# Experts' second products in 256, 304 or 384 columns, picked inside each product, instead of four whole-block forms

## The reference, cut to what matters

```python
scores = softmax(xf @ gate_w.T)            # 8 experts
weights, idx = top_k(scores, 2)            # two experts for each token
h  = einsum('td,eid->eti', xf, w1)         # 2048 -> 1024, each expert
g  = silu(h) * einsum('td,eid->eti', xf, w3)
eo = einsum('eti,edi->etd', g, w2)         # 1024 -> 2048
y  = sum over the two chosen experts of eo * weight
z  = silu(xf @ ws1.T) * (xf @ ws3.T) @ ws2.T   # the shared expert, all tokens
out = x + y + z
```

```
core 0  541 461 502 499 552 505 514 522
core 1  476 500 553 504 504 475 547 537
core 2  512 469 574 478 548 452 505 558
core 3  551 482 509 501 535 467 545 506
core 4  560 450 517 517 592 491 486 483
core 5  529 482 505 525 495 536 516 508
core 6  510 479 542 499 534 528 465 539
core 7  514 507 492 523 562 491 460 547
```

## The kernel before, in words

| rows | form | hidden columns | down tiles |
| --- | --- | --- | --- |
| up to 480 | 0 | one product of 480 | 4 |
| 481 to 512 | 1 | one product of 512 | 4 |
| 513 to 544 | 2 | two of 272 | 5 |
| over 544 | 3 | two of 320 | 5 |

## Time and profile before

### The profile page before, as it was taken

One profiled execution on the slowest core, in us unless ns is written; L12 is line 12 of the kernel. 1 busy time (PEld: TensorE's weight loads), 2 busy tenths in 40 slices (PEclk: granted clock), 3 DMA queues, 4 the chain that ended last, 5 costly groups with the idle time before them and its releaser, 6 DMA issues.

```text
span 2527.0 us, 41508 instructions; the slowest of 8 cores (2481.8 to 2527.0 us)
## 1 busy us (share of the span) xinstructions
PE 2262.4 (90%) x14499; PEld 1310.4 (52%) x14656; DVE 1055.5 (42%) x2142; ACT 710.4 (28%) x1332; POOL 323.8 (13%) x539
## 2 busy tenths in 40 slices
PE   5898999888997999989899999799599879989997
PEld 4555555455544655455444466356256534455443
DVE  5656665666556655555551222021011202111367
ACT  3444442345415553334312102021021202111000
POOL 1111110021101110011111010111011111110331
PEclk8999999999998999999899999899799989989999
DMA  6979887687747876686689698989988696995998
GB/s 101 186 165 214 173 167 176 173 158 128 129 137 172 146 128 119 206 167 121 116 243 225 155 234 159 182 180 178 232 154 176 141 189 144 202 214 119 221 302 320
DMA packets 110734, 445.42 MB, mean 176 GB/s; under 512 B 12416, under 2 KB 12432, under 8 KB 100368
## 3 DMA queue, kind: packets, MB, share of 16 engines
q0 software_dynamic: 76640, 278.47, 62.7%
q1 hardware_dynamic: 33840, 163.59, 18.3%
HBM read 577.84 MB, written 109.05 MB: 272 GB/s over the span
## 4 chain that ended last, share of the span: by engine, by line
PE 67%; DVE 9%; DMA 9%; issue 9%; ACT 5%; DVEq 1%; POOL 0%; ACTq 0%; SPq 0%; POOLq 0%
PE ps L717 24%; PE ps L752 13%; PE ps L446 10%; PE ps L454 7%; PE ps L420 6%; PE ps L431 5%; DVE FW L1101 3%; DMA out<-acc 2%; PE ps L644 1%; DMA gg<-eo,idx 1%; DMA xb<-x_own 1%; DVE Tt L1154 1%; DMA xp<-x_own 1%; DMA out<-y 1%; DMA acc<-y1d 1%
## 5 line engine op out<-in xcount | busy, mean ns | idle before, releaser
L717 PE MATMUL ps<-xg,wr 128*128 128x320 bf16 (+3 forms) x3066 | 488.7, 323 | 80.0 <-issue 76.7
L717 PEld LDWEIGHTS ps<-xg,wr 128*128 128x128 bf16 x3072 | 302.6, 99 | 265.1 <-issue 90.2
L431 PE MATMUL ps<-xT,wq 128*128 128x512 bf16 x978 | 254.7, 402 | 16.3 <-DVE lg L1185 9.8
L1414 DVE TENSOR_TENSOR gb<-sil,ps 128x320 bf16<-128x320 bf16 (+3 forms) x96 | 51.6, 538 | 507.7 <-PE ps L717 507.7
L1580 POOL DMA_DIRECT2D wr<-w_t x240 | 128.0, 546 | 958.2 <-PE ps L717 582.8
L752 PE MATMUL ps<-wr,gb 128*128 128x512 bf16 (+2 forms) x1128 | 247.5, 379 | 3.4 <-issue 1.3
L446 PE MATMUL ps<-wv,xT 128*128 128x256 bf16 x2048 | 232.0, 275 | 3.5 <-ACT xT L808 2.0
L420 PE MATMUL ps<-xT,wk 128*128 128x512 bf16 x983 | 224.4, 380 | 8.7 <-DVE qt L1166 5.0
L454 PE MATMUL ps<-wo,ob 128*128 128x512 bf16 x996 | 225.1, 381 | 2.8 <-issue 0.4
L1025 ACT ACTIVATE sil<-ps 128x320 bf16<-128x320 f32 (+3 forms) x128 | 64.8, 507 | 545.2 <-PE ps L717 535.2
L446 PEld LDWEIGHTS ps<-wv,xT 128*128 128x128 bf16 x2048 | 199.6, 99 | 29.0 <-issue 4.2
(11 more groups left out here) (159 smaller groups left out, 2427.7 us busy)
## 6 DMA issues: line engine op xcount, KB each, us to landing
wr<-w_t POOLq DMA_DIRECT2D x240, 512.0 KB, 19.5
wv<-wv_t POOLq DMA_DIRECT2D x64, 512.0 KB, 8.7
wk<-wk_t POOLq DMA_DIRECT2D x64, 512.0 KB, 10.1
wq<-wq_t POOLq DMA_DIRECT2D x64, 512.0 KB, 7.4
xs<-x2T SPq DMA_DIRECT2D x40, 512.0 KB, 15.0
y1d<-y SPq DMA_DIRECT2D x20, 1024.0 KB, 5.5
xst<-xs SPq DMA_DIRECT2D x40, 512.0 KB, 18.9
eo<-eos SPq DMA_DIRECT2D x40, 512.0 KB, 4.2
```

Of the source, the lines that this page charges most:

```text
L431: ins = t.matmul(self.ps[:, b, :], self.wq[i % 2][:, k * 128:(k + 1) * 128], self.xT[q % 2][:, k, :], start=(k == 0), stop=(k == 15))
L717: ins = t.matmul(self.ps[:, bk, 0:w], self.wr[c % NRING][:, k * 128:(k + 1) * 128], rhs, start=(k == 0), stop=(k == 15))
L1414: v.tensor_tensor(dst, self.sil[n // step % 2][:, 0:w], self.ps[:, self.bank[1, b, ic, s, f], 0:w], OP.mult).then_inc(self.v_g, step)
```

## The change

An expert's hidden columns are now split 256 + 384 in every engine's program, and there is one body for each block. TensorE's first product always has 256 columns. Each second product sits in a small branch (`pe_tail`): 256 columns for up to 512 rows, 304 for up to 560, 384 above. There are 16 such branches in a block, each with three alternatives of 16 matmuls. The gather and the first four down tiles are outside any branch; a fifth tile (`pe_fifth`) is either 32 matmuls or the four small ones. ScalarE and VectorE have no branch left; they always process 256 and 384 columns. The waits for the eight w2 chunks now stand together ahead of the first down product. The fifth tile always has 128 rows; before it had 32 or 128.

```diff
-BLOCKS += [(e, CAP // 128, [(0, CAP // 2), (CAP // 2, CAP // 2)]) for e in range(NX)]
+BLOCKS += [(e, CAP // 128, [(0, 256), (256, CAP - 256)]) for e in range(NX)]
-FORMS = [((0, 480),), ((0, 512),), ((0, 272), (272, 272)), ((0, 320), (320, 320))]
-FTILES = (4, 4, 5, 5)
+WIDTHS = (256, 304, CAP - 256)
...
         for b in range(NB):
+            if 0 < b < NB - 1:
+                self.count = count[b - 1]
+            self.pe_hidden(t, b, BLOCKS[b][2])
             if b == 0:
-                self.pe_hidden(t, b, 0, BLOCKS[b][2])
-                count = self.counts(t)
-                self.pe_xg(t, 0)
-                self.pe_down(t, b, BLOCKS[b][1])
-            elif b < NB - 1:
+                t.wait_ge(self.v_flag, 1)
+                count = [t.value_load(self.rows[0:1, e:e + 1]) for e in range(NX)]
+            if b < NX:
+                self.pe_xg(t, b)
+            self.pe_down(t, b)
+            if 0 < b < NB - 1:
+                mark = len(self.free8)
                 with t.If(count[b - 1] > 512):
-                    with t.If(count[b - 1] > 544):
-                        self.pe_block(t, b, 3)
-                    with t.Else():
-                        self.pe_block(t, b, 2)
+                    self.pe_fifth(t, b, True)
+                last = self.free8[mark:]
+                del self.free8[mark:]
                 with t.Else():
-                    with t.If(count[b - 1] > 480):
-                        self.pe_block(t, b, 1)
-                    with t.Else():
-                        self.pe_block(t, b, 0)
-                self.free8 += self.form8
...
-                    bk = self.take8(t, (wh, b, ic, s, f), (self.v_g, n) if wh else (self.a_sil, n))
+                    bk = self.take8(t, (wh, b, ic, s), (self.v_g, n) if wh else (self.a_sil, n))
+                    if s and 0 < b < NB - 1:
+                        with t.If(self.count > 256 + WIDTHS[0]):
+                            with t.If(self.count > 256 + WIDTHS[1]):
+                                self.pe_tail(t, b, c, wh, bk, WIDTHS[2])
+                            with t.Else():
+                                self.pe_tail(t, b, c, wh, bk, WIDTHS[1])
+                        with t.Else():
+                            self.pe_tail(t, b, c, wh, bk, WIDTHS[0])
+                        continue
...
+    def pe_tail(self, t, b, c, wh, bk, w):
+        for k in range(16):
+            ins = t.matmul(self.ps[:, bk, 0:w], self.wr[c % NRING][:, k * 128:(k + 1) * 128],
+                           self.xg[(b - 1) % 2][:, k, 256:256 + w], start=(k == 0), stop=(k == 15))
+        ins.then_inc(self.t_u3 if wh else self.t_h, 1)
...
         t.wait_ge(self.v_g, HN[b, 7, len(splits) - 1])
-        for tt in range(nt):
+        for ic in range(8):
+            c = 24 * b + 16 + ic
+            t.wait_ge(self.d_wr[c % NRING], 16 * (c // NRING + 1))
+        for tt in range(4 if nt == 5 else nt):
             for dg in range(4):
...
+    def pe_fifth(self, t, b, some):
+        for dg in range(4):
+            if some:
+                self.pe_y(t, b, 4, dg)
+                continue
+            m = (b - 1) * 10 + 8 + dg // 2 + 1
+            bk = self.take8(t, ("y", b, 4, dg), (self.v_eo, m) if dg % 2 else (self.a_eo, m))
+            c = 24 * b + 16
+            t.matmul(self.ps[:, bk, 0:8], self.gb[:, 0, 0:128], self.wr[c % NRING][:, 0:8],
+                     start=True, stop=True).then_inc(self.t_y, 1)
...
-    def act_sil(self, a, b, f, splits):
...
+            for ic in range(8):
+                for s, (off, w) in enumerate(splits):
+                    n = HN[b, ic, s]
+                    a.wait_ge(self.t_h, n)
+                    if n > 2:
+                        a.wait_ge(self.v_g, n - 2)
+                    a.activation(self.sil[n % 2][:, 0:w], self.ps[:, self.bank[0, b, ic, s], 0:w],
+                                 AF.Silu).then_inc(self.a_sil, 1)
...
-    def dve_gated(self, v, b, f, splits):
...
+                    v.tensor_tensor(dst, self.sil[n % 2][:, 0:w], self.ps[:, self.bank[1, b, ic, s], 0:w],
+                                    OP.mult).then_inc(self.v_g, 1)
```

More of the change, by code:

```diff
@@ L649, in pe_ffn @@
     def pe_ffn(self, t):
-        ps = self.ps
         nf = len(self.free)
@@ L725, in pe_down @@
+    def pe_down(self, t, b):
         nt, splits = BLOCKS[b][1], BLOCKS[b][2]
         t.wait_ge(self.v_g, HN[b, 7, len(splits) - 1])
-        for tt in range(nt):
+        for ic in range(8):
+            c = 24 * b + 16 + ic
+            t.wait_ge(self.d_wr[c % NRING], 16 * (c // NRING + 1))
+        for tt in range(4 if nt == 5 else nt):
             for dg in range(4):
[L729 to L754, removed]
@@ new lines, in pe_down, with pe_y @@
+                self.pe_y(t, b, tt, dg)
+    def pe_y(self, t, b, tt, dg):
+        n = YN[b, tt, dg]
+        if b == 0:
+            freed = (self.v_z, n)
+        elif b < NB - 1:
+            m = (b - 1) * 10 + tt * 2 + dg // 2 + 1
+            freed = (self.v_eo, m) if dg % 2 else (self.a_eo, m)
+        else:
+            freed = (self.v_cmb, n - YN[NB - 2, CAP // 128 - 1, 3])
+        bk = self.take8(t, ("y", b, tt, dg), freed)
+        for ic in range(8):
+            c = 24 * b + 16 + ic
+            if 0 < b < NB - 1:
+                lhs = self.gb[:, ic, tt * 128:(tt + 1) * 128]
+            else:
+                lhs = (self.g3 if b else self.g0)[tt // 4][:, ic, (tt % 4) * 128:(tt % 4 + 1) * 128]
+            ins = t.matmul(self.ps[:, bk, :], lhs, self.wr[c % NRING][:, dg * 512:(dg + 1) * 512],
+                           start=(ic == 0), stop=(ic == 7))
+        ins.then_inc(self.t_y, 1)
@@ L1013, in act_program @@
                 a.activation(self.fs[:, :], self.ps[:, 0, :], AF.Silu).then_inc(self.f_sil, 1)
-    def act_sil(self, a, b, f, splits):
[L1017 to L1028, removed]
     def act_ffn(self, a):
         for b, (e, nt, splits) in enumerate(BLOCKS):
[L1032 to L1046, removed]
+            for ic in range(8):
+                for s, (off, w) in enumerate(splits):
+                    n = HN[b, ic, s]
+                    a.wait_ge(self.t_h, n)
[3 more added lines that the diff above has]
+                                 AF.Silu).then_inc(self.a_sil, 1)
+                if b == 0 and ic < 3:
+                    self.act_left(a, 4, ic + 1)
             if b < NX:
@@ L1423, in dve_ffn @@
     def dve_ffn(self, v):
         for b, (e, nt, splits) in enumerate(BLOCKS):
-            if 0 < b < NB - 1:
-                with v.If(count[b - 1] > 512):
-                    with v.If(count[b - 1] > 544):
-                        self.dve_gated(v, b, 3, FORMS[3])
-                    with v.Else():
-                        self.dve_gated(v, b, 2, FORMS[2])
-                with v.Else():
-                    with v.If(count[b - 1] > 480):
-                        self.dve_gated(v, b, 1, FORMS[1])
-                    with v.Else():
-                        self.dve_gated(v, b, 0, FORMS[0])
-            else:
-                self.dve_gated(v, b, 0, splits)
-                if b == 0:
-                    count = self.counts(v)
+            for ic in range(8):
+                for s, (off, w) in enumerate(splits):
+                    n = HN[b, ic, s]
+                    v.wait_ge(self.a_sil, n)
+                    v.wait_ge(self.t_u3, n)
+                    dst = (self.gb[:, ic, off:off + w] if 0 < b < NB - 1
+                           else (self.g3 if b else self.g0)[s][:, ic, :])
+                    v.tensor_tensor(dst, self.sil[n % 2][:, 0:w], self.ps[:, self.bank[1, b, ic, s], 0:w],
+                                    OP.mult).then_inc(self.v_g, 1)
+                if b == 0 and ic < 3:
+                    self.dve_left(v, 4, ic + 1)
+                if b == NB - 1:
+                    for T in MIXES[ic]:
+                        self.dve_mix(v, T)
```

43 lines of the change are left out of this document (6 added, 37 removed).

## The result

The changed kernel takes 2471.74 us (median of 4 runs, 2465.21 to 2778.86) where the one before, timed beside it, takes 2538.36: a ratio of 0.9738, with a 95% interval of 0.9693 to 0.9783. The forecast was 2463 us, 3.1% under the median before; measured are 2.6%. The profiled execution took 2465.21 us. Its slowest core is not the one forecast (0) but 4, with 7 and 5 beside it. View of cores, after: microseconds from first to last instruction and mean granted clock, as in the earlier trace rows.

What follows compares the result with a forecast made beforehand. TensorE bounds, interrupted by code fetches after far jumps. Core 0: 2511.8 less 63.1 (jumps) and 11.6 (columns), with 12 (weights) and 8 (pages) 2457; 1.6 outside the span and 4 for the median give 2463 us; range 2432 to 2515.

Steps and rivals of the forecast that it cites:

- The far jumps: TensorE's gaps ahead of blocks are code fetches after far jumps; without them core 2 loses 86.0 us, core 0 63.1.
- rival D: Ahead of blocks: the gaps are not the jumps'; only columns would move, about 2528 us; chance 0.05.
- 8 us, some 6 of the sum hidden: Gaps ahead of core 2's blocks: a far jump costs about 8 us, some 6 hidden by queued matmuls.
- The near price: TensorE's remaining short jumps: 0 to 0.4 us each, as on VectorE, covered by queued matmuls.
- The columns: Hidden stages take 56.1, 61.1 or 69.7 us by row count; cores 0 and 2 each gain 11.6 us.
- What comes late instead: Expert blocks without pauses: weights may come late, 12 us taken, and code pages, 8 us taken.
- Rival B: Expert blocks: weights bound, gaps become ring waits; full 32 us and 15 more in block 9, 2498 us; chance 0.13.
- C: Hidden stages: each page fetched anew after a near jump, 8 us beyond some 4 of cover; 2730 us; chance 0.09.
- pages: Hidden stages: 8.6 code pages each, one in 6.6 us; late pages cost 0 to 48 us, 8 taken.
- come up to 1.5 us earlier than their use; nothing: Ahead of the down stage: grouping the waits for w2 chunks makes them up to 1.5 us early, at no cost.
- the same sum puts the six others lower: Cores other than 0 and 2 end earlier by the same subtraction; core 6 at 2427 us.
- take-back: Expert blocks: time lost again to late weights and late code pages, 12 + 8 us.

Runs made afterwards that it cites:

- the shortened blocks: Changed kernel with every second product 256 columns wide, no fifth tile and no branch, leaving out rows over 512: 2444.08 us, ratio 0.9645.
- the skipped code: Changed kernel with two more never-run alternatives of 32 matrix instructions in each of the 128 units: 2638.14 us, ratio 1.0391.
- the three-body kernel: Kernel before with the new columns, still in whole-block bodies with far jumps, three bodies for four: 2504.19 us, ratio 0.9884.
- spread and trimmed loads: Changed kernel with block 3's accumulator loads spread one to a block and unread fifth-tile rows not moved: 2453.24 to 2453.81 us, ratio 0.9677.
- the far kernel: Changed kernel with three jumps ahead of each expert block on TensorE, each over 768 never-run instructions: 2635.44 us, ratio 1.0400.

## Why the prediction was right, and where it was off

**The far jumps, right.** The cause was shown by putting them back: 160 us for 24 jumps at distance, 0.4 us for 24 near ones. No "issue" gap over 2.2 us is left in the expert blocks of any core, and rival D is out. The instruction queue brought 82 or 83 packets in the expert blocks of cores 0, 2 and 4 (about 90 forecast). The price fitted to core 2 was looser than the text says: by "8 us, some 6 of the sum hidden" its 3 jumps come to 18 us where 12.8 stand, a third stray. But over all cores the means of 2.0, 9.1, 15.1 and 26.1 us for 1 to 4 jumps lie near the 2, 10, 18 and 26 of that rate. The near price was taken at VectorE's 0 to 0.4 us with the matmul queue as cover; on TensorE it held.

**The columns, right for a stage without a gap.** 61.0 and 55.9 us measured, 61.1 and 56.1 forecast. The average stage is longer: 58.6 us for 256 columns (56.1 to 64.7, 34 stages) and 61.7 for 304 (27 stages), by the gaps inside and the slower matmuls behind them (3.51 us for 16 in the row at 1772.20). The slower ones also count as busy: core 0's products lost 6.9 us of busy time and not 11.6. The clock of the expert blocks, forecast at 1.00, was 0.99 to 1.00 on all cores.

**What comes late instead, right in sum.** For core 0 12 us of weight waits and 8 us of pages were taken; measured are 10.6 + 4.7 (the `eos` waits, themselves waits for stores) and 4.4; 3.9 more are the wait ahead of the last expert's down stage and small ones. That 740 us of traffic under 747 us of TensorE's work is nearly no slack was right: the share is 1.00, and the shortened blocks show the floor. Rivals B and C are both true mechanisms, each at its threshold here and hardly past it: the shortened blocks are B, the skipped code is C. Their named signs did appear, small: "issue" gaps 7 to 8 us apart inside hidden stages, 4 to 9 us a core in sum, and "DMA wr" waits ahead of down, 2 to 15 us a core. C's price of 8 us for each page was put on the wrong event, though: a near branch costs next to nothing extra; it is the pace of 6.5 us a page that costs, as the term "pages" of the sum had it. One step said that the w2 waits "come up to 1.5 us earlier than their use; nothing". Core 0's fourth block waited 10.59 us there in one piece; with the waits at their uses, in the kernel with the new columns in whole-block bodies, the same block waited 2.28 + 2.19 + 2.37 = 6.8 us. The 3.8 us between them may be this step's; it was not tried alone. A smaller part shows on every core: where a down stage waits for VectorE's last product, the first matmul starts 1.1 to 1.5 us after that product ends with the eight waits ahead of it, and 0.4 to 0.7 us after it with the waits at their uses (before, and in the three-body kernel). That is some 0.8 us each in the last expert's block and in block 9.

**Block 9, missed.** The sum let block 9 keep its length. The step that failed is "the same sum puts the six others lower": by it core 4 would end at 2506.6 - 72.9 - 0.7 = 2433 us, with the 20 us at 2453. Its take-back in the expert blocks was 19.6 as allowed, but block 9 grew by 9.5 (and it began the expert blocks 3.2 us later, and ran them in 2.2 us less than that sum): it ended at 2463.5. This is where the growth lies. On core 4, before and after, VectorE's last products and TensorE's first down matmuls of block 9 (the first row of TensorE's is cut by the end of the view):

```profile
2428.16 1.28 DVE L1414 TENSOR_TENSOR g<-sil,ps 128x512 bf16<-128x512 bf16 x2
...
2430.18 1.06 PE L752 MATMUL ps<-wr,g 128*128 128x512 bf16 x2 [4.93 <-DVE g L1414]
```

```profile
2382.99 1.28 DVE L1402 TENSOR_TENSOR g<-sil,ps 128x512 bf16<-128x512 bf16 x2
...
2385.40 22.57 PE L749 MATMUL ps<-wr,g 128*128 128x512 bf16 x96 [12.77 <-issue]
```

Measured from block 9's first matmul, the down stage starts 115.6 us later before and 123.4 after. The row says "issue", but VectorE's last `g` ends at 2382.99 + 1.28 = 2384.27, 1.1 us ahead of the first matmul (0.7 before): the eight chunk waits that now stand between hide the releaser. VectorE was late because it combines the experts' outputs between its `g` products, and waited for gathers. Its and POOL's waits from block 9's first matmul to its down stage, core 4, before and after:

```profile
DVE acc L1397 <- DMA gg<-eo,idx: 18.9, 2, 10.1
DVE y L1397 <- DMA gg<-eo,idx: 15.8, 3, 12.7
POOL gg L1549 <- DMA eo<-eos: 6.2, 1, 6.2
```

```profile
DVE acc L1386 <- DMA gg<-eo,idx: 23.9, 3, 12.1
DVE y L1386 <- DMA gg<-eo,idx: 19.8, 2, 16.6
POOL gg L1518 <- DMA eo<-eos: 10.2, 1, 10.2
```

The first gather is issued 17.2 us into the block instead of 11.8, behind a store that lands later. VectorE waits 43.7 us for gathers instead of 34.7, 9.0 us more, and TensorE's down stage starts 123.4 - 115.6 = 7.8 us later. That the one makes the other is read from the waits; no run moved the gathers alone. Over all eight cores the gap ahead of this down stage grew from 2.4 to 8.4 us on average. Rival B had "15 more in block 9 for pushed-back loads" in it; the place was right and the carrier was not: TensorE waits for VectorE there, and VectorE for gathers. With half of w2 gone in the expert blocks (block 9's own weights are whole) the gap is still 6.3 us on average (12.59 on core 4), and with spread and trimmed loads 7.9.

**Core 0's number, close in part by luck.** The sum gave core 0 2457 us and its span was 2453.2. But its expert blocks, forecast at 822.6 - 63.1 - 11.6 + 20 = 767.9 us, took 778.3: 10.4 more, by the columns (4.7), the take-back (3.6) and small terms. An earlier start of the blocks (8.5) and a shorter block 9 (5.8), neither forecast, hid that. The start varies by itself: the three profiled executions of the changed kernel have it at 1480.7, 1484.8 and 1483.5. In block 9 the down stage began later on core 0 too (121.2 us for 114.4), but from there to the end it took 73.1 us for 85.7; on the other cores that last part took 70 to 84 us in both kernels, and what sets it was not followed up. On core 0 VectorE's waits for loads of accumulators in that part fell from 20.7 to 10.4 us.

**The number.** 2471.7 against 2463: core 4 in place of core 0 makes 6.5 us of it (a span of 2463.5 against 2457), and the median lies 8.2 us over that span, where 1.6 + 4 had been allowed. Both are well inside the range of 2432 to 2515.

## What to carry to other kernels

Count the instructions that an engine's queue holds for each microsecond of work, skipped alternatives too: here a page of 256 needs 6.5 us, a jump over 768 instructions costs a page's wait and one over 32 next to nothing, and a small alternative costs little but its length. Before removing an engine's pauses, set the DMA traffic of the stretch against its new length; with 740 us in 747, the next gain lay in unread rows and in bursts. And write down, for each core, what the last stage waits for: with the stages before it shortened, another core and another engine's order of work may set the end.

## What the runs showed that was not expected

**Short code gaps lower the clock.** With far jumps put back, the first product after a gap took 3.57 us for 16 matmuls where 1.91 is usual, as at 1.2 instead of 2.4 GHz; core 4's granted clock was 0.90 in 1480 to 2430 us, and its hidden products were busy for 541.6 us against 520.7. With 151 us more of gaps that makes 172; its span grew by 168, with block 9 6.5 us shorter. With skipped code, gaps of at most 4.5 us did the same: on core 2 553.0 us against 519.5, at a granted clock of 0.97 in its expert blocks where it was 1.00. Not every such gap did it: in the stage of 1605 to 1687 us 16 matmuls took 1.91 us after a gap of 2.38 and 3.58 after one of 2.03. The rows of the far kernel, core 4:

```profile
1630.75 3.57 PE L713 MATMUL ps<-xg,wr 128*128 128x256 bf16 x16 [16.27 <-issue]
1637.07 2.95 PE L722 MATMUL ps<-xg,wr 128*128 128x256 bf16 x13 [2.12 <-issue]
```

**Cores in step may disturb each other.** The average gap ahead of block 9's down stage was 2.4 us before, where the eight cores enter the block within 49 us (each by the time since its own first instruction), 8.4 in the changed kernel (24 us), and 11.6 with the shortened blocks, where all enter within 7.5 us. In between the order is not clean: the three-body kernel has 4.9 us and the skipped-code one 8.1, both at 35.5. The cores compute nothing together, so something that they share may explain it, but no run moved the cores against each other and left the rest alone. It stays open.
